# A third image-row sample on TensorE, and the front of a chunk moved behind the MLP and into the attention

## What is computed

```
# layer 0: deformable convolution (4 groups of 32 channels, 9 points each), then an MLP
xp     = x @ w_in + b_in
h      = gelu(batchnorm(depthwise3x3(x)))
offset = h @ w_off + b_off            # 4 groups x 9 points x (x, y) per pixel
mask   = softmax over the 9 points of (h @ w_msk + b_msk)
y      = sum over points of mask * bilinear_sample(zero-padded xp, point + offset)
y      = y @ w_out + b_out
x      = x + gamma1 * layer_norm(y)
x      = x + gamma2 * layer_norm(gelu(x @ w_fc1 + b_fc1) @ w_fc2 + b_fc2)

# layer 1, tokens t = the 3136 pixels of an image
t = t + causal_attention(norm(t))     # one head of 128 channels
t = t + top2_of_8_experts(norm(t))
```

## Time and profile before

| | |
|---|---|
| median of 3 runs | 8632.43 us (8629.86 to 8637.22) |
| profiled execution: time | 8630.16 us |
| profiled execution: span, first to last instruction | 8628.4 us |
| mean granted TensorE clock | 0.826 of full speed |
| gathers (L696) | 6664, 34 for each of 196 tiles |
| dense matmul records (L1433) | 2240, 40 for each of 56 chunks |

### The profile page before, as it was taken

How to read it: one execution, slowest core, us unless ns; L and a number is a source line. 1 busy time by engine, 2 the same in 40 slices (tenths; PEclk the granted TensorE clock), 3 DMA queues, 4 the chain that set the end, 5 groups by cost and what they waited for, 6 DMA issues and landing times.

```text
span 8628.4 us, 76783 instructions
## 1 busy us (share of the span) xinstructions
PE 6134.7 (71%) x22738; PEld 3426.3 (40%) x22738; DVE 5230.7 (61%) x11181; ACT 3061.2 (35%) x6106; POOL 6354.4 (74%) x6703
## 2 busy tenths in 40 slices
PE   5557687767867687676777677776767676776667
PEld 3334344433444344443444334443434343343334
DVE  5656656656476655775466646666665755665453
ACT  2324333433334333433334333343333343333222
POOL 6777777777777777777777777777777777777770
PEclk8778788888878788888888888887888788887778
DMA  4222222222222222222222222222222222222220
GB/s 103 70 66 68 67 68 69 68 69 67 66 73 66 71 63 70 70 71 66 67 68 71 69 65 72 67 70 66 65 74 65 72 65 66 62 64 59 60 60 6
DMA packets 676666, 575.35 MB, mean 67 GB/s; under 512 B 392666, under 2 KB 569026, under 8 KB 676304
## 3 DMA queue, kind: packets, MB, share of 16 engines
q0 software_dynamic: 214928, 439.68, 18.7%
q1 hardware_dynamic: 460704, 130.97, 6.8%
q10 hardware_dynamic: 672, 0.24, 0.0%
HBM read 500.41 MB, written 69.97 MB: 66 GB/s over the span
## 4 chain that ended last, share of the span: by engine, by line
POOL 45%; PE 22%; issue 17%; DVE 11%; DMA 2%; ACT 2%; SPq 1%; POOLq 0%; DVEq 0%; another core or an unknown queue 0%; ACTq 0%
POOL ring L696 45%; PE bank L1433 4%; PE bank L1516 3%; PE bank L1551 3%; PE bank L1539 3%; DVE y L1049 2%; PE bank L1614 2%; PE bank L1702 2%; PE bank L1679 1%; DVE ring L1037 1%; DMA ring<-column_table,idx_r 1%; DMA tin<-tokens 1%; DMA tokens<-z 0%; SPq L507 0%; DVE z L1082 0%
## 5 line engine op out<-in xcount | busy, mean ns | idle before, releaser
L696 POOL DMA_INDIRECT ring<-column_table,idx_r x6664 | 6330.3, 950 | 2061.9 <-issue 2009.9
L1049 DVE TENSOR_REDUCE y<-ring 128x96 f32<-128x3456 f32 x196 | 1192.2, 6083 | 24.0 <-remote 21.6
L1037 DVE TENSOR_TENSOR ring<-ring,bank 128x4352 f32<-128x4352 f32 x196 | 917.8, 4683 | 391.7 <-POOLq L707 390.0
L1516 PE MATMUL bank<-kT,qT 128*112 128x448 f32 (+3 forms) x1792 | 788.2, 588 | 108.2 <-DVE cmax L1160 72.7
L1433 PE MATMUL bank<-arena,stripes 116*128 116x448 f32 (+1 forms) x1792 | 786.0, 555 | 21.3 <-ACT arena L784 21.1
L1551 PE MATMUL bank<-pT,xh 112*128 112x448 f32 (+3 forms) x1792 | 775.8, 516 | 0.2
L1160 DVE TENSOR_REDUCE cmax<-bank 112x1 f32<-112x448 f32 (+3 forms) x896 | 508.6, 580 | 408.5 <-PE bank L1516 296.0
L1539 PE MATMUL bank<-qT,kT 128*112 128x448 f32 (+3 forms) x1792 | 754.5, 506 | 1.2 <-ACT qT L833 1.2
L1503 PE MATMUL bank<-ident,xh 112*128 112x112 f32 x224 | 56.4, 408 | 973.7 <-DVE xh L967 973.7
L839 ACT ACTIVATE pT<-bank 112x448 f32<-112x448 f32 (+3 forms) x896 | 451.3, 504 | 696.3 <-PE bank L1539 496.1
L1131 DVE TENSOR_TENSOR part<-bank,part 128x448 f32<-128x448 f32 x112 | 69.9, 624 | 992.1 <-PE bank L1433 935.8
(11 more groups left out here) (193 smaller groups left out, 8203.1 us busy)
## 6 DMA issues: line engine op xcount, KB each, us to landing
ring<-column_table,idx_r POOLq DMA_INDIRECT x6664
column_table<-proj SPq DMA_DIRECT2D x196, 112.0 KB
corner_weight<-wts_s SPq DMA_DIRECT2D x56, 252.0 KB, 3.3
wts_r<-corner_weight SPq DMA_DIRECT2D x196, 72.0 KB
tin<-tokens SPq DMA_DIRECT2D x56, 224.0 KB, 3.0
out<-xn SPq DMA_DIRECT2D x56, 224.0 KB, 2.6
xin<-in_x SPq DMA_DIRECT2D x49, 224.0 KB, 3.1
x<-in_x SPq DMA_DIRECT2D x28, 256.0 KB, 3.9
```

Source lines behind the costliest of these rows:

```text
L696: pool.indirect_dma_start(ring[:, r, e * CORNERS:(e + 1) * CORNERS, :].rearrange("p s c -> p (s c)"), None, source, bass.IndirectOffsetOnA ...
L1037: dve.tensor_tensor(corners, corners, wts_p.unsqueeze(2).broadcast_to([128, FETCHED * CORNERS, CG]), ALU.mult)\
L1049: step.did(dve.tensor_reduce(y[:, k % BLK % 2, 0:(G - 1) * CG].rearrange("p (g c) -> p g c", c=CG), terms[:, 0:whole].rearrange("p (g e) c ...
L1516: ins = pe.matmul(scores[0:TT, 0:n], qT[:, q * TT:(q + 1) * TT], kT[:, c, 0:n], start=True, stop=(c < j))
```

## The change

`DENSE` goes from 2 to 3, so that 33 samples are gathered and three come from image rows. The experts and the front are no longer one step: `front` (x turned, convolution, gelu, projection, logits) runs ahead of the attention, behind the MLP of the earlier half; `front_rest` (the mask's exponentials, storing of corners) and VectorE's parts of the front run inside the attention. The hats have three pairs of buffers, all in `arena`, and `front_positions` is split into `read_logits` and `find_corners`. The logits now lie in bank 1.

```diff
-DENSE = 2
+DENSE = 3
-PLACE_BANKS = ((3, 6), (4, 5))
-SUM_BANKS = (0, 4)
+HAT_PAIRS = 3
+PLACE_BANKS = ((3, 6), (4, 5), (3, 6))
+SUM_BANKS = (0, 4, 0)
...
-        def hats_ahead(j):
-            return max(STAGES, ITEMS + 1 - blocks(j))
+        def items_by(j, b):
+            last = min(blocks(j) - 1, ITEMS - STAGES)
+            return STAGES + (ITEMS - STAGES) * min(b, last) // last
...
@@ timeline @@
+                        ahead = (p, fronts[h]) if live[h] else None
+                        if ahead:
+                            front(ahead, 2 * s + h, g if att else 0)
                         if att:
-                            attention(i, j, h, s, (p, fronts[h]), first, second, now)
+                            attention(i, j, h, s, (p, fronts[h]), first, second, now, ahead)
+                            experts((i, j), third, 2 * s + h)
                         else:
+                            front_rest(ahead)
                             tile(*first)
                             tile(*second)
                             dense(now)
-                        experts_front((i, j) if att else None, (p, fronts[h]) if live[h] else None, third,
-                                      2 * s + h, g if att else 0, now)
+                            tile(*third)
...
@@ ACT, hats @@
-                act.wait_ge(d_summed, FIRST + gd * (NB * DENSE) + 2 * max(item - STAGES + 1, 0))
-                pair = hats2[stage]
+                act.wait_ge(d_summed, FIRST + gd * (NB * DENSE) + 2 * max(item - HAT_PAIRS + 1, 0))
+                pair = hats2[item % HAT_PAIRS]
...
@@ ACT, attention @@
+                if ahead:
+                    front_rest(ahead)
                 if now:
                     act.wait_ge(experts_read, FIRST + g)
                     widen_weights(gd, 0)
-                    for item in range(ahead):
+                    for item in range(STAGES):
                         hats(gd, item)
...
@@ VectorE, attention @@
+                if ahead:
+                    keep_projections(ahead)
                 layer_norm(tin[:, buf], xh[:, NT * j:NT * (j + 1)], NT, TT, 1e-5, 1).then_inc(xn_made, 1)
+                if ahead:
+                    p, f = ahead
+                    read_logits(2 * p + f // NJ, f % NJ)
                 if now:
-                    set_places(dense_chunk(*now)[2])
+                    for d in range(DENSE):
+                        set_place(dense_chunk(*now)[2], d)
...
                 if second:
                     multiply(*second)
+                if ahead:
+                    find_corners(2 * p + f // NJ, f % NJ)
+                if now:
+                    keep_part(*now, 0)
+                if second:
                     sum_up(*second)
+                if ahead:
+                    front_weights(2 * p + f // NJ, f % NJ)
                 if now:
-                    keep_part(*now)
+                    for d in range(1, DENSE):
+                        keep_part(*now, d)
...
@@ PE, attention @@
-                banks_left(fronts, s * 2 + h, g)
-                if now:
-                    spread_rows(gd)
                 if first:
                     tile(*first)
+                if ahead:
+                    fp, ff = ahead
+                    pe.wait_ge(f_proj_kept, FIRST + turned(fp, ff + 1))
+                else:
+                    banks_left(fronts, s * 2 + h, g)
+                if now:
+                    for d in range(2):
+                        spread_rows(gd, d)
...
+                if ahead:
+                    pe.wait_ge(f_logits_read, FIRST + fp * (2 * NJ) + ff + 1)
                 pe.matmul(bank[1][:, 0:CH], wa[:, :], kT[:, j], start=True, stop=True).then_inc(q_made, 1)
+                if now:
+                    spread_rows(gd, 2)
...
-                    if now and 1 <= b <= ITEMS - ahead:
-                        sum_columns(di, gd, ahead + b - 1)
+                    if now and b:
+                        for item in range(items_by(j, b - 1), items_by(j, b)):
+                            sum_columns(di, gd, item)
...
@@ PE @@
+            def front(ahead, s, n_att):
+                p, f = ahead
+                fi, fj = 2 * p + f // NJ, f % NJ
+                banks_left(ahead, s, n_att)
+                for c in turned_in(fi, fj):
+                    pe.wait_ge(f_hidden, FIRST + fi * NJ + fj)
+                    turn_x(fi, c)
...
+                convolve(fi, fj)
+                for c in turned_in(fi, fj):
+                    project_x(fi, c)
+                find_logits(fi, fj)
+
+            def experts(unit, third, s):
+                i, j = unit
+                g = i * NJ + j
+                pe.wait_ge(t1_made, FIRST + g * NT + NT)
+                pe.wait_ge(xm_made, FIRST + g + 1)
+                pe.wait_ge(d_kept, FIRST + dense_done(s + 2))
```

More of the change, by code:

```diff
@@ L424, in fronts_done, with timeline @@
             return p, f
-        def timeline(eng, first_image, tile, attention, experts_front, mlp, dense):
+        def timeline(eng, first_image, tile, front, front_rest, attention, experts, mlp, dense):
             def attended(p, a):
@@ L470, in timeline @@
             for f in range(1, LEAD):
[L471 removed]
+                front((0, f), 0, 0)
+                front_rest((0, f))
             tile(0, 0, 0)
@@ L610, in tile, with attention @@
                 ring_load(p, t)
-            def attention(i, j, h, s, fronts, first, second, now):
+            def attention(i, j, h, s, fronts, first, second, now, ahead):
                 if first:
@@ L637, in mlp @@
                 sp.dma_start(tin[:, half], tok_pair[s, half]).then_inc(tok_in[half], 16)
-            def experts_front(unit, ahead, third, s, n_att, now):
-                if ahead:
-                    front(*ahead)
+            def experts(unit, third, s):
+                i, j = unit
                 if third:
                     tile(*third)
[L644 to L650, removed]
+                sp.wait_ge(o_made, FIRST + i * NJ + j + 1)
+                sp.sem_inc(passed, 1)
+                sp.dma_start(out_ch[i, j], o[:, :, :]).then_inc(o_out, 16)
+            timeline(sp, first_image, tile, front, front_rest, attention, experts, mlp, dense)
             sp.wait_ge(o_out, PRIMED + 16 * N * NJ)
@@ L928, in _ @@
+            timeline(act, first_image, tile, front, front_rest, attention, experts, mlp, dense)
         @block.vector
@@ L1136, in dense, with attention @@
-            def dense(now):
-                set_places(dense_chunk(*now)[2])
-                keep_part(*now)
-            def attention(i, j, h, s, fronts, first, second, now):
+                    keep_part(*now, d)
+            def attention(i, j, h, s, fronts, first, second, now, ahead):
                 g = i * NJ + j
@@ L1530, in attention @@
                     spread_weights(gd, 0)
-                    for item in range(NT, ahead):
+                    for item in range(NT, STAGES):
                         sum_columns(di, gd, item)
@@ new lines, in front_rest, with experts @@
+            def front_rest(ahead):
+                pass
+            def experts(unit, third, s):
+                i, j = unit
+                g = i * NJ + j
+                pe.wait_ge(t1_made, FIRST + g * NT + NT)
+                pe.wait_ge(xm_made, FIRST + g + 1)
+                pe.wait_ge(d_kept, FIRST + dense_done(s + 2))
+                for t in range(NT):
+                    ins = pe.transpose(bank[0][:, t * TT:(t + 1) * TT], xn[:, t, :], ident[0:TT, 0:TT])
+                ins.then_inc(xm_turned, 1)
```

293 lines of the change are left out of this document (134 added, 159 removed).

## The result

| | time, median | to the kernel before on the same chip |
|---|---|---|
| before | 8634.1 us (8629.9 to 8637.2) | |
| changed | 8747.2 us (8743.0 to 8758.3) | 1.0134 [1.0121, 1.0147] |
| changed, ScalarE's hats one item earlier | 8546.2 us (8540.9 to 8557.1) | 0.9897 [0.988, 0.9913], against 8637.2 us on that chip |

The change makes the kernel 1.3% slower, where 1.1% faster was forecast. The third row is the experiment that finds the cause: on ScalarE a hat's instructions come one item earlier, and nothing else differs.

A forecast was written before the change was run, and what follows sets the result against it. The gathers bound the kernel, the rest only 3.6% faster; 7437 + 114 + 62 = 7613 us from 887 gives 8500, plus 30 of waits, 1.8 and 2.3: 8535 us (-1.1%), range 8400 to 8665.

The forecast's parts named there:

- What bounds before, and the ceiling: POOL's gathers, 1.255 us apart, set the time; dropping one of 34 gains at most 246 us, to 8384.
- Rest of the kernel: All but the gathers, served without delay from 911.8 us on: 7717 less 280 us of VectorE's waits, 7437 us.
- Experts: Last attention projection to last expert sum, with the front taken out: 10.4 us less a unit.
- From the MLP to attention: Second MLP result to attention, where the front now runs: 2.1 us more a unit.
- the price that was bounded from outside: The front's convolution after PE idles: 9.2 us taken, between 6.8 at high clock and 13.6 at low.
- Rival B: Slower: the front misfits the gap after the MLP at low PE clock, 8724 us; sign: gap above 21 us; chance 0.17.
- Start of attention to the maxima: Logits' reading, a third placing and a row-spread wait go ahead of VectorE's sum: 3.2 us more a unit.
- The transposed scores: Five more dense items and four weight transposes on PE: 7.95 us more in six chunks of seven, 11 in chunk 0.
- The 7.95: Transposed scores outside chunk 0: 7.55 us for five more dense items, 0.4 for four more weight transposes.
- A: POOL's gathers stay the bound because the loss terms are half as large: 8390 to 8440 us; chance 0.2.
- C: No change to speak of, 8615 to 8650 us: the ring does not smooth short and long units; chance 0.06.
- D: Gathers slow down as VectorE's added work hits POOL's issue; sign: pace over 1.279 us; chance 0.02.

The follow-up runs named there:

- the move alone: The changed kernel's order of work with two image-row samples and 34 gathers, as before: 8624.4 us (0.9988); with every second gather left out from tile 25, 8071.9 us.
- ahead_only: The changed kernel with ScalarE's hats one item earlier and nothing else: 8546.2 us, 0.9897 to the kernel before; with half the gathers 8530.0 us.
- edit 3: The changed kernel with PE transposing the next dense sample's weights before the block's dense matmuls, not behind them: 8606.0 us, 0.9969 to the kernel before.

## Why the prediction was wrong

**What bounds before, and the ceiling: right.** The gathers bounded it, one gather less is worth 246 us only if the rest keeps up, and the rest did not. "Rest of the kernel" was put at 8350, from the start; it is 8399.5, since 230 of the 280 us of VectorE's waits went when the gathers were halved: a unit lost 3.6 of its 4.4 us of waits, in units 47 to 53 10.8 of 13.2. Counting the waits in full cost 49 us.

**Experts: right.** -10.7 for -10.4. Unit 19, 45.9 us before, takes 31.9 now, from the first line to the end of the second:

```profile
3287.30 1.13 PE L1617 MATMUL bank<-wv,xnT 128*112 128x129 f32 x8 [0.63 <-ACT xnT L866]
...
3317.15 2.00 PE L1742 MATMUL bank<-arena,ident 112*112 112x128 f32 x16
```

**From the MLP to attention: right**, +1.6 for +2.1, and with it the price that was bounded from outside: the convolution took 8.70 us in unit 34 (9.2 taken, bounds 6.8 and 13.6). Rival B, the only one on the slower side, set its place here and is out: the gap is 17.7 us, its mark was 21.

```profile
5465.75 8.70 PE L1667 MATMUL bank<-xpad,diag 128*128 128x448 f32 x18 [1.13 <-ACT xflat L877]
...
5481.03 0.60 PE L1551 MATMUL bank<-ident,xh 112*128 112x112 f32 x4 [1.56 <-DVE xh L987]
```

**Start of attention to the maxima: right for most units, missed for seven.** +3.2 for 2.7. In units 47 to 53, which have no logits to read, I counted 1.1 and it is +3.4 (26.8 to 30.2). The move alone leaves that stretch at 26.9 there, so all of it is the third sample: its row spread (L1453) stands on PE behind q's projection, and VectorE waits for it ahead of its sum (unit 49):

```profile
7785.37 0.68 DVE L1133 TENSOR_SCALAR xflat<-bank,dcol 116x448 f32<-116x448 f32 x1 [2.59 <-PE bank L1453]
```

**The transposed scores: the step that failed.** The words were: "ACT makes a hat in 2.19 us and an exponential in about 0.5, under the 3.02 us that PE needs per block, so three hats in flight instead of five should do." The number of buffers was indeed harmless (38.0 to 38.1 in the move alone, and ahead_only keeps three pairs). But a rate says nothing on when the first hat comes. 2.19 + 0.5 fits into 3.02; the first hat of the loop has two keepings of 0.54 us and two widenings of 0.62 us ahead of it besides the exponentials, and is wanted in the block in which it is begun. PE waited for it before as well, in the row at 5471.07, which the prediction left out of its account. The third sample put its weights behind that wait, and what was 1.3 us a unit (38.0 to 36.7) became 4.1 (50.0 to 45.9). That was the larger part of the term's miss: the stretch grew by 12.0 us a unit where 8.4 were counted.

The 7.95 itself: with hats one item earlier in both, the third sample lengthens the stretch from 36.9 to 45.9 us, by 9.0, of which chunk 0 12.0 (19.4 to 31.4; 11 counted) and chunk 3, as an example of the others, 8.6 (36.7 to 45.3; 7.95 counted). That ahead_only lands on 45.9, the forecast's 38.0 + 8.4 less 0.5, is thus two errors that cancel: a baseline with a hidden 1.1 us of waiting (38.0 for 36.9), and a term short by 0.6 (8.4 for 9.0). Part of the 0.6 is the 0.42 us wait for the exponential above; the rest stays open. That ahead_only as a whole, 8546, is near the forecast of 8535 is of the same kind.

**The sum.** From 8535 to 8747 are 212 us, here from the kernel before with half its gathers to the changed one: 49 from the baseline; 142 from units 4 to 46 (256 for the 114 counted), where the transposed scores alone are 3.6 us a unit over their term and the others nearly cancel; 45 from units 47 to 53 (107 for the 62 counted), by the same term and the start of attention; 11 from the beginning, since unit 0 starts 31 us later (354.7 for 323.4) and the units 0 to 3 win back 45, 14 us sooner in all, where the prediction had 25; -3 at the last two units; -30 for waits on gathers that never came. They add up to 214, 2 of it rounding.

**The rivals.** A (gathers stay the bound) and C (the ring does not smooth) fall with VectorE's missing waits. D (gathers slow down) falls by the group of the gathers, whose mean is what it was:

```profile
L713 POOL DMA_INDIRECT ring<-column_table,idx_r x6468 | 6144.6, 950 | 2312.5 <-issue 1926.4 <-DMA wts_r<-corner_weight 350.4 <-DMA ring<-column_table,idx_r 35.7
```

950 ns, as on the page of before. By D's own mark alone (1.279 us from one start to the next) it would have come true, since the mean is 1.303 (8482.0 - 53.1, over 6468). But 350.4 us of that are POOL's waits for ring loads, which D did not mean; without them it is 1.249.

The rule of the Trainium skill on the port pair (SBUF - State Buffer), which the prediction set against the rows, does not show here either. What happened was none of the rivals: slower, but by a late operand in the term that I had called PE time that nothing covers. That B's price of 8724 lies near the 8747 measured is chance. None of the prediction's three signs of being wrong came up either (POOL waited 350.4 us, the gap is 17.7, VectorE waits for no gather): each was the mark of a rival that it had thought of. The range ended at 8665 because its only slow case was put into another stretch.

## What to carry to other kernels

Where two engines pass work to and fro in a fixed order, compare not only their rates but, for the first item of the loop, the time at which it is begun with the block that wants it; then look up the consumer's wait at that very place in the trace of before, even if it is small and the engine is not the bound. A slack that is hidden under one bound (63 us of late hats under the gathers) is paid once the bound moves, and anything queued behind it multiplies it. Halving the bounding work in both kernels gives the length of the rest in two runs, and should come before any discussion of terms.

## What was not expected of the hardware

- The same late operand had two prices. Behind a wait of 1.88 us of PE the granted clock fell in unit 34 (0.57 over 4 us) and stayed at 1.00 in unit 16, where PE was as busy in the 4 us around the wait (2.12 us); over the 46 units outside chunk 0 it fell in 25. Behind waits of 1.36 us (the kernel before) and 1.50 (edit 3) in the same units it never fell. What decides in the changed kernel is open.
- Edit 3, a mere reordering on PE, won 141 of the 201 us and left the first wait at 1.49 us. It took away the second wait, 0.4 us of the first, and every fall of the clock in this stretch outside chunk 0. In the 21 units in which the clock had not fallen the stretch became 2.0 us shorter, in the 25 others 3.3 us: here too the waits are the larger part.
- The convolution behind the MLP was no dearer than between attention and router: its records average 634 ns in the changed kernel and 607 in ahead_only, 648 in the kernel before.
